# A cross-attention and feed-forward block on one core: three in-order engines take up their per-slot work in another order

## The reference, cut to what matters

```python
x = x + mlstm(layernorm(x), ctx, ctx, ...)      # 16 batch elements of 128 x 128, 8 heads of 16
    # gates -> log_f, cumulative sum, running max -> D_mat = exp(log_D - max_log_D)
    # C = (q k^T / sqrt(16)) * D_mat ; o = C v ; h = o / (max(|sum C|, exp(-max)) + eps)
    # layernorm of h over 128, times ln_scale
x = x + ffn(layernorm(x))                       # 128 -> 512 -> 512 -> 128, weights +1/-1, relu
```

## Time and profile before

| | |
|---|---|
| median of 3 runs | 140.13 us (139.77 to 140.87) |
| the profiled execution | 140.68 us, of which 138.9 us are the span from the first to the last instruction |
| mean granted TensorE clock | 0.956 of full speed |
| busy | PE 112.5 us, DVE 95.9, ACT 74.7, POOL 70.0 |

### The profile page before, as it was taken

How to read it: one execution, slowest core, us unless ns; L and a number is a source line. 1 busy time by engine, 2 the same in 40 slices (tenths; PEclk the granted TensorE clock), 3 DMA queues, 4 the chain that set the end, 5 groups by cost and what they waited for, 6 DMA issues and landing times. The chain is left out here.

```text
span 138.9 us, 3358 instructions
## 1 busy us (share of the span) xinstructions
PE 112.5 (81%) x1141; PEld 83.7 (60%) x1141; DVE 95.9 (69%) x294; ACT 74.7 (54%) x173; POOL 70.0 (50%) x143
## 2 busy tenths in 40 slices
PE   4899999993998299979969698698888858769861
PEld 4777668562955185575827467376474656658751
DVE  5685595879689685809994994985898546471631
ACT  3026675974676464379649717835744631374230
POOL 5592675188784786654665777553214032520000
PEclk9999999999599959999999999999999977999997
DMA  3482190149683774635284753737001000101001
GB/s 104 138 224 49 39 258 15 42 60 183 121 151 61 161 132 66 134 54 101 19 189 76 156 105 88 147 38 159 2 5 38 0 5 0 38 0 38 17 26 38
DMA packets 12992, 11.38 MB, mean 82 GB/s; under 512 B 2080, under 2 KB 11440, under 8 KB 12976
## 3 DMA queue, kind: packets, MB, share of 16 engines
q0 software_dynamic: 1728, 6.29, 25.3%
q1 hardware_dynamic: 10112, 4.53, 12.7%
q10 hardware_dynamic: 1136, 0.35, 1.0%
HBM read 8.94 MB, written 1.25 MB: 73 GB/s over the span
## 5 line engine op out<-in xcount | busy, mean ns | idle before, releaser
L453 PE MATMUL pF<-h,w 128*128 128x256 f16 x256 | 31.1, 277 | 0.0
L643 ACT ACTIVATE h<-pF 128x512 f16<-128x512 f32 x32 | 18.1, 594 | 22.9 <-PE pF L453 22.9
L870 DVE SCALAR_TENSOR_TENSOR h<-pF,h 128x512 f16<-128x512 f32 x32 | 21.1, 681 | 9.5 <-ACT h L643 9.5
L453 PEld LDWEIGHTS pF<-h,w 128*128 128x128 f16 x256 | 25.1, 100 | 3.1
L1017 POOL TENSOR_SCALAR ve_hx<-mv_hx 128x2 f32<-128x2 f32 (+1 forms) x17 | 4.0, 236 | 32.8 <-DVE mv_hx L828 31.7
L783 DVE SCALAR_TENSOR_TENSOR cmat<-pS,dmat 128x1024 f32<-128x1024 f32 x15 | 18.2, 1216 | 2.1 <-PE pS L379 2.1
L379 PE MATMUL pS<-q_heads,qcT 64*128 64x512 f32 x64 | 18.1, 641 | 0.3 <-DVE cmat L783 0.3
L996 POOL TENSOR_SCALAR_AFFINE_SELECT maxb<-aT 128x1024 f32<-128x1024 f32 x12 | 13.2, 1102 | 4.4 <-ACT em L573 4.4
L412 PE MATMUL pX<-ident,x2p 128*128 128x128 f16 x32 | 4.4, 217 | 13.6 <-POOL x2p L1029 13.4
L796 DVE SCALAR_TENSOR_TENSOR den<-pO,em 128x8 f32<-128x8 f32 x16 | 2.6, 164 | 17.1 <-PE pO L400 17.1
L1018 POOL TENSOR_TENSOR rs_hx<-ve_hx,minus_half 128x2 f32<-128x2 f32 (+1 forms) x17 | 13.0, 766 | 1.4
(11 more groups left out here) (124 smaller groups left out, 211.5 us busy)
## 6 DMA issues: line engine op xcount, KB each, us to landing
maxb<-running_max POOLq DMA_DIRECT2D x12, 512.0 KB, 5.3
out<-outb SPq DMA_DIRECT2D x8, 128.0 KB, 1.8
xs<-in_x SPq DMA_DIRECT2D x3, 256.0 KB, 7.2
cs_in<-in_ctx SPq DMA_DIRECT2D x3, 256.0 KB, 7.6
q_heads<-qcT SPq DMA_DIRECT2D x24, 32.0 KB, 2.7
xs<-in_x SPq DMA_DIRECT2D x2, 128.0 KB, 3.2
cs_in<-in_ctx ACTq DMA_DIRECT2D x1, 256.0 KB, 3.7
k_in<-in_L_ffn_k SPq DMA_DIRECT2D x1, 256.0 KB, 3.8
```

The source lines that it names most:

```text
L453: last = pe.matmul(bank[:, u], w1[:, k, columns], h1[:, k, part], start=(k == 0 and part == 0), stop=(k == FT - 1 and part == 1))
L643: act.activation(hidden(f, m, 0), ffn_place(f, m), ACT.Relu).then_inc(ffn_high, 1)
L870: dve.scalar_tensor_tensor(out=hidden(f, m, 1), in0=ffn_place(f, m), scalar=0.0, in1=hidden(f, m, 0), op0=ALU.max, op1=ALU.subtract).then_ ...
```

## The change

On SP, the loads of x and context of group 2 are issued only when context group 0 and x group 1 have landed. On PE, `turn_o(n-1)` stands ahead of the units, `turn_late_xn` behind the early unit, and of the 15 products that nobody reads in slots 3 to 5 there remain 6, ahead of `turn_o`. On DVE the product stands between two low parts, the residual and its statistics ahead of the normalizer, and a group of four normalizations in slot 1 ahead of the gate scans. On POOL `hx_scale` moves to the next slot, behind `x2_take_low`. ACT is as before.

```diff
--- before.py
+++ after.py
@@ -269,6 +269,8 @@
                 sp.dma_start(bias_in[:, n:n + 1], bias.rearrange("(h a) -> h a", a=1)).then_inc(gatew_loaded, 16)
             load_x(1)
             load_ctx(1)
+            sp.wait_ge(ctx_loaded[0], 16)
+            sp.wait_ge(x_loaded[1], 16)
             load_x(2)
             load_ctx(2)
 
@@ -512,25 +514,25 @@
                     turn_late_ctx(g + 2)
                 if 0 <= n - 1 < B:
                     weigh(n - 1)
-                if 0 <= n - 4 < B:
-                    turn_x2(n - 4)
-                if k == 3 and g + 2 < NG:
-                    turn_late_xn(g + 2)
-                for f, m in early:
-                    ffn(f, m)
                 if 2 <= n + 1 < DIRECT:
                     spread_never(n + 1)
                     spread_max(n + 1, 0)
                     spread_max(n + 1, 1)
+                if 0 <= n - 4 < B:
+                    turn_x2(n - 4)
+                if 3 <= n <= FFN_LAG:
+                    pe.wait_ge(exp_ready, DIRECT)
+                    keep_busy(2)
                 if 0 <= n - 1 < B:
                     turn_o(n - 1)
+                for f, m in early:
+                    ffn(f, m)
+                if k == 3 and g + 2 < NG:
+                    turn_late_xn(g + 2)
                 for f, m in late:
                     ffn(f, m)
                 if n == 1:
                     turn_am(1)
-                if 3 <= n <= FFN_LAG:
-                    pe.wait_ge(exp_ready, DIRECT)
-                    keep_busy(5)
 
         @block.scalar
         def _(act):
@@ -918,31 +920,31 @@
                 early, late = ffn_of_slot(n)
                 behind = 0 <= n - 1 < B
                 behind_2 = 0 <= n - 2 < B
-                for f, m in before:
+                for f, m in before[:1]:
                     low(f, m)
                 if n < B:
                     make_c(n)
+                for f, m in before[1:]:
+                    low(f, m)
+                if behind_2:
+                    residual(n - 2)
+                    x_at = x_statistics(n - 2)
                 if n == 0:
                     q_span(2 * GB, GB)
                     q_span(3 * GB, GB)
                 if n == 1:
+                    norm_group(2)
                     gate_scans(1)
                 if prepare and k == 0 and n > 0:
                     gate_scans(g + 1)
-                if behind:
-                    at = normalizer_1(n - 1)
                 if n >= 2:
                     norm_q(n + 3 * GB - 2)
                 if behind_2:
-                    residual(n - 2)
+                    x_moments(n - 2, x_at)
                 if behind:
+                    at = normalizer_1(n - 1)
                     at = normalizer_2(n - 1, at)
-                if behind_2:
-                    x_at = x_statistics(n - 2)
-                if behind:
                     at = normalizer_3(n - 1, at)
-                if behind_2:
-                    x_moments(n - 2, x_at)
                 if behind:
                     head_out(n - 1, at)
                     at = h_statistics(n - 1)
@@ -952,8 +954,6 @@
                     low(f, m)
                 if behind:
                     h_centred(n - 1)
-                if n == 1:
-                    norm_group(2)
                 if n == 3:
                     ffn_weights_0_2()
 
@@ -1074,10 +1074,10 @@
             for n in range(SLOTS):
                 if 0 <= n - 4 < B:
                     x2_take_low(n - 4)
+                if 0 <= n - 2 < B + 1:
+                    hx_scale(n - 1)
                 place(n + LEAD)
                 take_values(n + GB)
-                if 0 <= n - 1 < B + 1:
-                    hx_scale(n)
 
 
 # ---- launch ----
```

## The result

The changed kernel takes **131.12 us** in the median of 4 runs (130.65 to 131.61); the kernel before, beside it on the same chip, 140.12 (139.77 to 140.87). The ratio is 0.935, with a 95% interval of 0.930 to 0.940. The forecast was 131.5 us, in a range of 129.2 to 136.2.

A forecast was written before the change was run, and what follows sets the result against it. TensorE was taken as the bound, paying each slot for one inversion in POOL's list. Terms -3.0 - 4.0 + 0.5 + 0.75 + 1.0 - 0.6 - 3.9 + 0.6 = -8.65 from 140.68, less 0.55: 131.5 us, range 129.2 to 136.2.

The forecast's parts named there:

- Even slots, -0.85, and the last sum, -0.5: Even slots end 0.85 us sooner, three in slots 10 to 15; the 0.49 us wait before element 15's sum goes: -3.0.
- The new wait of 0.4: In every slot PE waits some 0.4 us for ACT's copy before the early turn of o, formerly hidden by a unit.
- Slots 1 to 5, -4.0: Slot 5 loses a 1.94 us wait and unread products; DVE's earlier normalizations and waiting residual cancel: -4.0, bounds -2.5 and -4.8.
- slot 5 near 6.5: A sign that the forecast is right: slot 5, 9.15 us long before, comes near 6.5 us.
- Slot 6, +0.5: Scale and placing stand between casts and low part, and unit (0, 1)'s second low part is behind the product: +0.5 us.
- Slots 7 and 8, +1.75: Late turn of x makes L445 wait for two ACT copies, +0.75; slot 8 waits for the copy of o, +1.0.
- The tail, -3.9: From element 15's sum to element 14's turn, 12.71 us become 8.8, the low part no longer waiting for scales: -3.9.
- DVE's order and the port: Product between lows free; DVE 10.0 us busy per two slots against PE's 10.5; port shared with POOL's placing costs +0.6 us.
- Rival A: DVE becomes the bound through the port shared with POOL, each meeting costing 0.74 us: 135.0 us; chance 0.22.
- Rival B: The wait only moves: the turn of o waits 1.2 us for ACT in each slot, 140 us; chance 0.07.
- Rival C: Slower: scales wait for ACT's cast and the residual delays the normalizer, a loop over four engines, 144.7 us; chance 0.04.
- Rival D: With nine unread products fewer, PE falls to 1.2 GHz more often; four more such units, 134.7 us; chance 0.07.

The follow-up runs named there:

- The exchange alone: The kernel before with only POOL's list changed, the low part of x2 ahead of the scales (`hx_scale`): 124.56 us, ratio 0.896.
- the best version: Kernel before plus POOL's low part ahead of scales, late turn of x, earlier normalizations, five unread products ahead of the turn of o: 125.52 us, ratio 0.899.

## Why the prediction was right, and where it was not

**What bounds the kernel** was right: half of PE's 26.4 us of idle time was one inversion in POOL's list. The exchange alone takes PE's wait for the low part from 13.4 us to 1.1, and the time down by 14.7; that is more than the wait, and the granted clock rose as well, from 0.956 to 0.985.

**Even slots, -0.85, and the last sum, -0.5**: -0.85 and, with the odd slots' small gain, -3.54 for -3.0. The new wait of 0.4 measured 0.28, the turn and all else as worked out. But the sum was made against the old slot alone. It showed what the early turn leaves, not that it costs 0.5 us in every slot against leaving it where it stood: in the exchange alone an even slot takes 4.7 us and not 5.2. Nothing in my terms priced the exchange without the other parts, so I took for the gain of the whole what was a gain of some 15 less a loss of some 6. The total was right all the same, because the sum described the whole list as it would stand.

**Slots 1 to 5, -4.0**: -3.46, of which slot 5 gave 3.32 (9.15 to 5.83 us). The wait went as said. The sign "slot 5 near 6.5" doesn't go with this term, which makes it 5.1; nor do the bounds named for the range, which add up to 129.1 and 134.2 and not to 129.3 and 133.5. That the fewer unread products bring 2 us was not borne out: putting them back cost 0.8 to 1.4, and taking them out of the exchange alone gained nothing. I take it that much of what they took was time in which PE would otherwise have waited; no run shows that by itself. That the earlier normalizations and the wait of the residual cancel was nearly so: slots 0 to 4 went from 27.15 to 27.01 us.

**Slot 6, +0.5**: +2.10, **the step that failed outright**. It rests on the sentence that the product between two low parts is free, the second being needed only halfway through L453. It is needed after 4 of 16 products. In slot 6 of the changed kernel:

```profile
50.28 0.60 PE L455 MATMUL pF<-h,w 128*128 128x256 f16 x4 [0.20 <-DVE h L872]
51.92 1.48 PE L455 MATMUL pF<-h,w 128*128 128x256 f16 x12 [1.04 <-DVE h L872]
```

The other waits of PE in that slot are 0.36 us for the low part of x2, for which the +0.5 allowed, and 0.47 before the sum; the four add up to 2.07 of the 2.10. The loop shows the cause of the largest: `u == 0 and k % FU == 0` asks for the second low part at k = 2 of the first column block, which is a quarter of the unit. In the later slots of the changed kernel the wait is hidden, since the early turn of o delays L455 by 0.5 us: two costs that cover one another, which is why the parts cost 4.4 and 4.3 alone and not 8.7 together.

**Slots 7 and 8, +1.75**: +1.38. The chain of two copies is there:

```profile
58.77 0.59 ACT L549 COPY qcT<-pG 128x512 f32<-128x512 f32 x1 [2.22 <-PE pG L318]
59.26 0.59 ACT L637 COPY x2T<-pX 128x512 f16<-128x512 f16 x1
59.73 1.07 ACT L610 ACTIVATE dmat<-maxb 128x1024 f32<-128x1024 f32 x1
59.99 1.03 PE L447 MATMUL pF<-x2T,w 128*128 128x256 f16 x8 [1.25 <-ACT x2T L637]
```

Slot 7 measured +0.87 for +0.75, slot 8 +0.51 for +1.0: the wait there was 0.61 us and not 1.2, ACT being no further behind by then.

**The tail, -3.9**: -3.94, and its clock rose from 0.87 to 1.00 as said.

**DVE's order and the port.** DVE's 10.0 us of busy time for two slots, the middle between two bounds, measured 9.67 in the changed kernel (slots 11 and 12, 8.96 before), whose pair takes 10.39: there it is slack. Behind the exchange PE alone would need 9.41, and the pair takes 10.04 with DVE busy 9.56. So DVE's list is then the tighter one, through the waits of L453 and of the sum. The residual, all 16:

```profile
L847 DVE SCALAR_TENSOR_TENSOR x<-hsc,rs_hx,xs x16: 335/343/1091, 29.3 to 110.5; 128x128 f32<-128x128 f32 x16
```

Its mean went from 397 to 432 ns, 0.56 us in all. That is the 0.6 that I put down, though as DVE time and not on the path. Rival A, the port at its full price in every slot, is refuted. The two do meet in eleven slots, but mostly at the end of the placing, which takes 1.09 us:

```profile
55.74 1.09 POOL L996 TENSOR_SCALAR_AFFINE_SELECT maxb<-aT 128x1024 f32<-128x1024 f32 x1
56.22 0.76 DVE L847 SCALAR_TENSOR_TENSOR x<-hsc,rs_hx,xs 128x128 f32<-128x128 f32 x1
```

Begun 0.14, 0.48 and twice 0.75 us into it, the residual took 1.09, 0.76 and 0.48 us, each time until 0.14 or 0.15 after its end; begun 0.91 or later, 0.34. Twice the residual came first, and the placing took 1.18. That the one waits for the other agrees with the Trainium skill's page "SBUF — State Buffer", section "Who interferes with whom".

**Rival B** (1.2 us of wait in each slot) fell: 0.28 in most, 0.61 at most. **Rival C** fell as a loop of every slot, but its mechanism is there once: DVE waits 2.8 us for the scales in slot 2, where that wait stands ahead of a normalizer that was ready, and PE's sum in slot 3 waits 0.9 us longer for the quotient than before. **Rival D** fell: the mean clock rose from 0.956 to 0.972. In slots 3 and 4 it was 0.77 and 0.66, though, against 0.81 and 1.00 before.

**The start**, foretold as 0, gave -1.74 in the profiled execution. No part of the change but SP's waits comes before it, and without them no longer time is shown. Two things differ there. One is the pace of PE's transposes behind the wait for the biases, first before, then after:

```profile
7.13 1.06 PE L311 MATMUL pG<-ident,cs_in 128*128 128x128 f32 x4
```

```profile
6.57 0.60 PE L313 MATMUL pG<-ident,cs_in 128*128 128x128 f32 x4
```

The same four transposes at about half the pace, although both executions had idled only half a microsecond or less just before. The other is DVE's second pair of normalizations, for which PE's next transposes wait:

```profile
7.40 0.97 DVE L740 TENSOR_SCALAR xn<-xs,mv_q,rs_q 128x128 f32<-128x128 f32 x2
```

```profile
6.90 0.60 DVE L742 TENSOR_SCALAR xn<-xs,mv_q,rs_q 128x128 f32<-128x128 f32 x2
```

In six of the 14 executions, the kernel before among them, it began at 7.04 us or later and took 0.97 to 1.41 us, until POOL's clearing of a 128x1024 tile beside it (7.27 to 8.23 in the kernel before) was over; in the other eight it began by 6.99 and took 0.60. None of the four kernels with SP's waits is among the six, which single executions don't make an effect. So 1.7 of the 10 us between the two profiled executions are most likely luck of the start; by the rows the rest of the change gave 8.3 us for the 8.65 forecast. That the forecast came within 0.4 us of the median is luck in part too: slot 6 lost 1.6 more than said, slots 1 to 5 gained 0.5 less, and slots 7 to 15, the start and a port whose price PE never saw made up for more than that.

**What stays open.** Not tried was whether the best version's parts would gain if the clock fell less in slot 5, nor was it found what lets the clock fall in slot 3 of one execution and in slot 5 of another, what decides the pace of the start, and whether SP's waits bear on it. The losses of the residual's place in slots 2 and 3 and in the steady slots were told apart only by the slot starts of one execution.

## What to carry to other kernels

When one wait is half of an engine's idle time, look at what stands ahead of its releaser in the releaser's own list, and time that one exchange alone before anything else: here it gave 14.7 us, and the rest of the edit took about 6 back. A step that needs a copy by another engine belongs behind a unit that needs nothing, even if it could start earlier; moved ahead, it shows the whole latency, once a slot. Price each part against the kernel as it will be with the other parts, not as it was: DVE's half microsecond a slot was slack against slots of 5.2 us and in the way against 4.7.

## What the runs showed of the hardware that I had not expected

TensorE's pace between 6 and 9 us of a launch differs from execution to execution by a factor of nearly two: the same four transposes took 1.06 us in six of the 14 and 0.60 in eight. Where DVE's normalizations were early, the first scores came at 13.94 to 14.36 us with the faster pace and at 14.99 to 15.10 with the slower; where they were late, at 14.85 to 16.69. The granted clock from 5.5 to 9 us stood at 1.00 in all 14, so that figure alone doesn't show the pace.

POOL is held up as DVE is: its low part took 429 ns in the mean before, 553 with its exchange alone, with single ones of 0.73 us. It now runs beside DVE's quotient, statistics and centred h; which of them holds it up is not shown. PE doesn't wait longer for it.
